# Alternating the PSUM bank of a unit's first dense item in a linear-attention phase

## The chip, the cores and the metric

The kernel runs on one core of one Trainium2 chip. The metric is the device time of one launch in microseconds, over the whole program: mixing, attention, MLP and routed experts. Before the change it is 2922.16 us, the median of three runs (2916.29 to 2923.81).

## What is computed

The input has 16 sequences of 512 tokens. A token mixing makes `h` from `x`; then a transformer block with linear attention, then a mixture of experts, each added to `h`. The change lies in the attention, whose core per sequence is (16 heads of 64, width 256):

```
h = _ln(x, g1, beta1)
q = _phi((h @ wq).reshape(b, s, H, DH), proj)      # elu(x @ proj) + 1
k = _phi((h @ wk).reshape(b, s, H, DH), proj)
v = (h @ wv).reshape(b, s, H, DH)
# causal: kv and ksum run along the tokens
num = q_t . kv ;  den = q_t . ksum + 1e-06 ;  out = num / den
x = x + out @ wo
```

## The kernel before

The program has three phases. `attention_phase` ends near 1,668 us, the MLP phase follows, and the routed experts end it. Only the first is touched. Every fp32 operand is split there into a high and a low fp16 part, and `three` (L498 to L502) makes each product of three matmuls, so the `nh`/`nl` in a row are the high and low part of the normalised rows, `sh`/`sl` those of the masked scores, `vh`/`vl` those of the values.

**The pipeline.** A *unit* is half a sequence, 256 tokens (`u = (i, h)`, two chunks `c` of 128 tokens), so there are 32 units. While unit u does its attention, the dense items of the *next* unit are computed and the mixing and norm of the unit after that. `unit` has eight slots `s`, and every engine runs the same list of steps (`run`), each doing its own part of a step in this fixed order. Nothing is scheduled at run time; engines meet at semaphores.

**The dense items.** The table `DENSE` spreads 13 items over the eight slots: eight feature items `f0` to `f7` (queries and keys, 12 matmuls of 256 columns each), four value items `v0` to `v3` (6 matmuls of 512 columns) and the output projection `p`. An item fills one of two PSUM banks, `pF[0]` and `pF[1]`, in turn: `n % 2`, with `n` counted through the table by `dense`. The count starts at 0 in each unit. As 13 is odd, `v3` (n = 12, slot 7) and the next unit's `f0` (n = 0, slot 0) are both in bank 0. Before an item is written, TensorE waits in `bank_free` until the item before it in its bank was read: a feature item is read by ScalarE (`rz`, L719) and last by VectorE (`fz`, L825), a value item by ScalarE (`vh`, L731) and last by VectorE (`vl`, L834).

**The boundary between two units** is where the change acts. TensorE's order there is: in slot 7 `v3`, the outputs (`pO`), a transposition (`pT`), the scores (`pS`, released by `sm` L851) and, where there is one, a state sum (`pKV`); then in slot 0 of the next unit `f0`, and the outputs of its first quarter. These outputs have two parts: a product with the state (`pO<-kvh,qkh`), which only chunks 1 to 3 have, and the product of values and masked scores (`pO<-vh,sh`), which waits for `sh`, for both parts of `sl` (VectorE's is L858) and for the values. VectorE's order in the same stretch is: in slot 7 `vl` of `v3`, division of the outputs (`dn`, `rd`, `on`; L875 to L883), the mask of the scores (`sm`, L851), the state (`kvt`, `kvacc`), then `sl` (L858). One slot earlier, at s = 6, it makes the norm's `tn` (L809) and `nl` (L815), with ScalarE's `nh` (L710) between; `f0` waits for both:

```
if n == 0:
    pe.wait_ge(nh_ready, units(w, DT, DT))
    pe.wait_ge(nl_ready, units(w, DT, DT))
bank_free(w, before)
```

I call the boundary inside a sequence (from unit (i, 0) to (i, 1)) A, and that between two sequences (from (i, 1) to (i + 1, 0)) B. At A the outputs have the state part and there is a state sum; at B neither.

Of the kernel before, what the change touches and what calls it, by code (L numbers as in the profile page):

```python
# [16 lines left out]
SEQS = 16  # L17
D = 256
DT = D // P
# [8 lines left out]
HALF = T // 2  # L28
XS = XK // 2
FEATS = 8  # L30
QK_GROUPS = 2 * QT * DT // 4
VALS = 4
# [3 lines left out]

DENSE = ((("f", 0),), (("f", 1), ("f", 2)), (("p", 0), ("f", 3)), (("v", 0), ("v", 1)), (("f", 4),),
         (("f", 5), ("f", 6)), (("f", 7), ("v", 2)), (("v", 3),))
OUT_BANK = 1
TURNS = 6 * CH - 2  # L40
EXP_LN_SET = 6
EXP_LN_SET = 6
# [4 lines left out]
WO_SCALE = 64.0  # L47
# [14 lines left out]
def after(u, n):  # L62

    return u[0] + (u[1] + n) // 2, (u[1] + n) % 2
# [27 lines left out]
def attention_phase(nc, io, w1_w, w2_w, mlp_loaded):  # L92
# [3 lines left out]
    with ExitStack() as ctx:  # L96
        def sb(name, shape, dt=F32):
            return ctx.enter_context(nc.sbuf_tensor(name, [P, *shape], dt))
# [8 lines left out]
        wo_h, wo_l = sb("wo_h", [QT, D], F16), sb("wo_l", [QT, D], F16)  # L107
# [142 lines left out]
        at = sb("at", [DT, HALF])  # L250

        def bank(name, dt=F32):
            return ctx.enter_context(nc.psum_tensor(name, [P, 2048 // (4 if dt == F32 else 2)], dt))

        pM = bank("pM")
        pF = [bank("pF0"), bank("pF1")]
# [43 lines left out]
        def run(engine, steps):  # L300


            def step(name, *args):
                if name in steps:
                    steps[name](*args)

            def use(u, what, bank, before):


                kind, n = what  # L310
                if kind == "p":
                    step("project", after(u, -1), before)
                elif kind == "f":
                    step("features", after(u, 1), n, bank, before)
                else:
                    step("values", after(u, 1), n, bank, before)

            def finish(u, what, bank):
                if what[0] == "f":
                    step("phi", after(u, 1), what[1], bank)  # L320
                elif what[0] == "p":
                    step("project_read", after(u, -1))

            def norm(u, s):

                if s < XS:
                    step("mix", u, s)
                    if s < XS - 1:
                        step("split", u, s + 1)
                    else:  # L330
                        step("h", u)
                elif s == 5:
                    step("x0", u)

            def norm_early(u, s):

                if s == 4:
                    step("mean", u)
                    step("centre", u)
                elif s == 5:  # L340
                    step("var", u)
                    step("rstd", u)
                elif s == 6:
                    step("normed", u)

            def dense(first, last):


                slots, before, n = [], {0: ("v", VALS - 1, 1), 1: ("f", FEATS - 1, 1)}, 0
                for s in range(8):  # L350
                    uses = [], []
                    for place, (kind, k) in enumerate(DENSE[s]):
                        if not ((kind == "p" and first) or (kind != "p" and last)):
                            uses[place].append(((kind, k), n % 2, before[n % 2]))
                            before[n % 2] = (kind, k, 0)
                        n += 1
                    slots.append(uses)
                return slots

            def unit(u, start=False, mix=True, last=False):  # L360
                i, h = u
                slots = dense(start, last)
                if mix:
                    step("split", after(u, 2), 0)
                for s in range(8):
                    c, g = 2 * h + s // 4, s % 4
                    early, late = slots[s]

                    summed = (c, g - 2) if g >= 2 and c < CH - 1 else (c - 1, g + 2) if g < 2 and c > 0 else None

                    if g < 2:
                        quad = (i, c, g + 2)
                    elif c < CH - 1:
                        quad = (i, c + 1, g - 2)
                    else:
                        quad = None if last else (i + 1, 0, g - 2)
                    for what in early:
                        use(u, *what)
                    step("outputs", i, c, g)

                    if g >= 2:
                        step("turn", i, c, g - 2)
                    elif c > 0:
                        step("turn", i, c - 1, g + 2)
                    elif not start:
                        step("turn", i - 1, CH - 1, g + 2)
                    for what in early:
                        finish(u, *what[:2])
                    if quad is not None:
                        step("scores", *quad)  # L390
                    step("outputs_split", i, c, g)
                    for what in late:
                        use(u, *what)
                    if summed is not None:
                        step("sums", i, *summed)
                    if g in (1, 2) and c < CH - 1:
                        step("keys", i, c, g - 1)
                    if quad is not None:
                        step("scores_split", *quad)
                    if summed is not None:  # L400
                        step("sums_split", i, *summed)
                    if mix:
                        norm_early(after(u, 2), s)
                        norm(after(u, 2), s)
                    for what in late:
                        finish(u, *what[:2])

            step("split", (0, 0), 0)
            for s in range(8):
                norm_early((0, 0), s)  # L410
                norm((0, 0), s)
            step("split", (0, 1), 0)
            slots = dense(True, False)
            for s in range(8):
                for what, bank_no, before in slots[s][0] + slots[s][1]:
                    use((0, -1), what, bank_no, before)
                    finish((0, -1), what, bank_no)
                norm_early((0, 1), s)
                norm((0, 1), s)
            for q in range(2):  # L420
                step("scores", 0, 0, q)
                step("scores_split", 0, 0, q)
            unit((0, 0), start=True)
            unit((0, 1))
            for i in range(1, SEQS - 1):
                unit((i, 0))
                unit((i, 1))
            unit((SEQS - 1, 0), mix=False)
            unit((SEQS - 1, 1), mix=False, last=True)
            step("turn", SEQS - 1, CH - 1, 2)  # L430
            step("turn", SEQS - 1, CH - 1, 3)
            step("project", (SEQS - 1, 1), ("p", 0, 1))
            step("project_read", (SEQS - 1, 1))

        block = ctx.enter_context(nc.Block())

# [60 lines left out]
        def _(pe):  # L497
            def three(out, wh, wl, mh, ml, first, last):  # L498

                pe.matmul(out, wh, mh, start=first, stop=False, skip_group_check=True)  # L500
                pe.matmul(out, wl, mh, start=False, stop=False, skip_group_check=True)  # L501
                return pe.matmul(out, wh, ml, start=False, stop=last, skip_group_check=True)  # L502

            def half(u):
                return slice(u[1] * HALF, (u[1] + 1) * HALF)
# [56 lines left out]
                               t == 0, t == DT - 1)  # L562
                mm.then_inc(v_done, 1)

            def project(u, before):
                bank_free(after(u, 2 - before[2] * (before[0] == "p")), before)
                pe.wait_ge(turn_read, output_turn(u[0], 2 * u[1] + 1, 3))
                for m in range(DT):
                    cols = slice(m * P, (m + 1) * P)
                    for t in range(QT):  # L570
                        mm = three(pF[OUT_BANK][:, m * HALF:(m + 1) * HALF], wo_h[:, t, cols], wo_l[:, t, cols],
                                   ot[:, 0, t, half(u)], ot[:, 1, t, half(u)], m == t == 0, t == QT - 1)
                mm.then_inc(at_done, 1)

# [206 lines left out]
        def _(ve):  # L781
# [53 lines left out]
                                               1 / V_SCALE, vh[:, c, heads, 0:DH],  # L835
                                               ALU.mult, ALU.subtract).then_inc(vl_ready, 1)

            def project_read(u):
                ve.wait_ge(at_done, units(u, 1, 1))
                if some(units(u, 1, 0)):  # L840
                    ve.wait_ge(at_stored, units(u, 16, 0))
                nc.vector.tensor_scalar(at[:, :, :], pF[OUT_BANK][:, :].rearrange("p (m n) -> p m n", m=DT), 1 / WO_SCALE, None,
                                        ALU.mult).then_inc(at_ready, 1)

            def scores(i, c, q):
# [1371 lines left out]
```

## Time and profile before

| | us |
|---|---|
| median of 3 runs (lowest, highest) | 2922.16 (2916.29, 2923.81) |
| the profiled execution | 2922.25 |
| its span in the trace | 2920.5 |
| TensorE busy | 2442.1 (84%) |
| VectorE busy | 1981.8 (68%) |
| GpSimd busy | 1665.0 (57%) |
| ScalarE busy | 1471.2 (50%) |

PE is TensorE (PEld its weight loads), DVE VectorE, ACT ScalarE, POOL GpSimd. A row's line is that of the code; matmuls all have the lines of `three`, so they are told apart by the tiles they write. "Idle before" is what the engine stood still before an instruction, with the releaser behind the arrow; the releaser "issue" means that the profile shows no semaphore event for it. PEclk is the granted clock of TensorE as a share of 2.4 GHz: 1.00 is that level, 0.50 is 1.2 GHz.

### The profile page before, as it was taken

The numbers are of one execution on the slowest core, as the hardware profiler recorded it, in microseconds if no ns is written. First come the engines' busy times: TensorE is split into PE (matmuls) and PEld (weight loads), VectorE is DVE, ScalarE is ACT, GpSimd is POOL, SyncE is SP. The second block draws the span as 40 slices with busy tenths as digits, with TensorE's granted clock in tenths as the row PEclk, the third lists the DMA queues.
The fourth block names the chain that finished last, engine by engine and source line by source line (L and its number), as shares of the span: only waits on it lengthen the run. The fifth ranks groups of instructions, "written<-read, shape, count | busy, mean of one in ns | idle before, by whom it ended". The sixth has DMA issues, their size and how long they took to land. (4 is left out here: it accounts for less than half of the span.)

```text
span 2920.5 us, 61365 instructions
## 1 busy us (share of the span) xinstructions
PE 2442.1 (84%) x22832; PEld 1757.8 (60%) x22832; DVE 1981.8 (68%) x4227; ACT 1471.2 (50%) x2731; POOL 1665.0 (57%) x1627
## 2 busy tenths in 40 slices
PE   4899999999999999999999759888888888955444
PEld 3677777877787778777877524444444444434333
DVE  3667777777777777777777538777877787852222
ACT  3656666666656566656666434444444344311111
POOL 1555556565655555555555324556556556657776
PEclk8999999999999999999999879999999999987666
DMA  4111111111111111111110121112112111004554
GB/s 141 38 41 38 35 44 34 41 38 41 38 42 34 45 34 41 34 45 34 42 38 16 35 72 59 37 41 69 37 37 72 39 37 51 16 22 99 86 87 64
DMA packets 110742, 138.14 MB, mean 47 GB/s; under 512 B 20720, under 2 KB 77040, under 8 KB 110448
## 3 DMA queue, kind: packets, MB, share of 16 engines
q1 hardware_dynamic: 84816, 110.94, 12.3%
q0 software_dynamic: 23552, 21.17, 4.7%
q8 instruction: 185, 3.03, 0.5%
q10 hardware_dynamic: 2080, 2.10, 0.2%
q14 instruction: 109, 0.89, 0.1%
HBM read 81.22 MB, written 53.04 MB: 46 GB/s over the span
## 5 line engine op out<-in xcount | busy, mean ns | idle before, releaser
L929 POOL TENSOR_TENSOR qkl<-fz,qkh 128x512 f16<-128x512 f32 x256 | 297.1, 1160 | 282.1 <-DVE qkh L828 282.1
L500 PE MATMUL pF<-nh,qk_h 128*128 128x256 f16 x1024 | 289.2, 282 | 62.7 <-DVE vl L834 57.2
L941 POOL TENSOR_TENSOR ol<-on,oh 128x256 f16<-128x256 f32 x256 | 188.4, 736 | 208.5 <-ACT oh L765 208.5
L1802 POOL DMA_INDIRECT list_dram<-entry,slot_u x256 | 257.4, 1005 | 75.3 <-issue 74.8
L502 PE MATMUL pF<-nl,qk_h 128*128 128x256 f16 x1024 | 289.2, 282 | 0.0
L501 PE MATMUL pF<-nh,qk_l 128*128 128x256 f16 x1024 | 289.1, 282 | 0.0
L749 ACT ACTIVATE ot<-pT 128x512 f16<-128x512 f16 x256 | 149.9, 586 | 182.8 <-PE pT L659 182.8
L742 ACT ACTIVATE sh<-sm 128x512 f16<-128x512 f32 x256 | 159.5, 623 | 105.6 <-DVE sm L851 105.6
L948 POOL TENSOR_TENSOR kvl<-kvacc,kvh 128x260 f16<-128x260 f32 x192 | 156.9, 817 | 91.3 <-ACT kvh L773 89.9
L1783 POOL TENSOR_TENSOR al<-az,ah 128x512 f16<-128x512 f32 x64 | 79.1, 1236 | 224.1 <-DVE ah L1575 224.0
L875 DVE TENSOR_SCALAR dn<-pO 128x4 f32<-128x4 f32 x256 | 40.4, 158 | 233.0 <-PE pO L502 232.8
L825 DVE SCALAR_TENSOR_TENSOR fz<-pF,ez 128x512 f32<-128x512 f32 x256 | 174.8, 683 | 34.8 <-ACT ez L725 33.3
L935 POOL TENSOR_TENSOR sl<-sm,sh 128x512 f16<-128x512 f32 x128 | 153.7, 1200 | 75.4 <-ACT sh L742 75.4
L719 ACT ACTIVATE rz<-pF 128x512 f32<-128x512 f32 x256 | 151.1, 590 | 83.1 <-PE pF L502 81.8
L500 PE MATMUL pS<-qkh 64*128 64x128 f16 x1024 | 189.0, 220 | 2.6 <-DVE sm L851 2.6
L501 PE MATMUL pS<-qkh,qkl 64*128 64x128 f16 x1024 | 186.4, 218 | 0.0
L502 PE MATMUL pS<-qkl,qkh 64*128 64x128 f16 x1024 | 186.3, 218 | 0.0
L851 DVE TENSOR_TENSOR sm<-pS,mask 128x512 f32<-128x512 f32 x256 | 174.3, 681 | 5.2 <-PE pS L502 5.2
L923 POOL TENSOR_TENSOR xl<-xs,xh 128x512 f16<-128x512 f32 x128 | 148.0, 1157 | 37.4 <-ACT xh L674 37.3
L725 ACT ACTIVATE ez<-rz 128x512 f32<-128x512 f32 x256 | 161.3, 630 | 8.2
L500 PEld LDWEIGHTS pF<-nh,qk_h 128*128 128x128 f16 x1024 | 102.7, 100 | 92.3 <-issue 61.6
L828 DVE CAST qkh<-fz 128x512 f16<-128x512 f32 x256 | 148.5, 580 | 8.8
(320 smaller groups left out, 8897.7 us busy)
## 6 DMA issues: line engine op xcount, KB each, us to landing
xs<-in_x SPq DMA_DIRECT2D x128, 256.0 KB, 2.7
h_dram<-hT SPq DMA_DIRECT2D x32, 256.0 KB, 2.2
x_dram<-x SPq DMA_DIRECT2D x32, 256.0 KB, 2.2
at_dram<-at SPq DMA_DIRECT2D x32, 256.0 KB, 2.2
x0b<-x_dram SPq DMA_DIRECT2D x16, 512.0 KB, 4.5
atb<-at_dram SPq DMA_DIRECT2D x16, 512.0 KB, 5.6
hb_in<-h_dram SPq DMA_DIRECT2D x16, 512.0 KB
xrow_dram<-xt SPq DMA_DIRECT2D x32, 256.0 KB, 2.2
```

Of the source, the lines that this page charges most:

```text
L500: pe.matmul(out, wh, mh, start=first, stop=False, skip_group_check=True)
L501: pe.matmul(out, wl, mh, start=False, stop=False, skip_group_check=True)
L502: return pe.matmul(out, wh, ml, start=False, stop=last, skip_group_check=True)
L725: nc.scalar.activation(ez[:, s, :, :], rz[:, s, :, :], ACT.Exp, scale=-1.0, bias=-math.log(PHI_DOWN)).then_inc(e_ready, 1)
L742: nc.scalar.activation(sh[:, q, :, :], sm[:, n % 2, :, :], ACT.Copy).then_inc(sh_ready, 1)
L825: nc.vector.scalar_tensor_tensor(fz[:, s, :, :], pF[bank_no][:, :].rearrange("p (b n) -> p b n", b=2), 0.0, ez[:, s, :, :], ALU.max, ALU.a ...
L851: nc.vector.tensor_tensor(sm[:, n % 2, :, :], pS[:, :].rearrange("p (a b) -> p a b", b=P), mask[:, :].unsqueeze(1).broadcast_to([P, 4, P]) ...
L929: nc.gpsimd.tensor_tensor(qkl[:, pair:pair + 2, cols], fz[:, n % 2, :, :], qkh[:, pair:pair + 2, cols], ALU.subtract).then_inc(fl_ready, 1)
L935: nc.gpsimd.tensor_tensor(sl[:, q, :, :], sm[:, 0, :, :], sh[:, q, :, :], ALU.subtract).then_inc(sl_ready[0], 1)
L941: nc.gpsimd.tensor_tensor(ol[:, n % 2, :], on[:, n % 2, :, :].rearrange("p a b -> p (a b)"), oh[:, n % 2, :], ALU.subtract).then_inc(ol_re ...
L948: nc.gpsimd.tensor_tensor(kvl[:, pairs, :, :], kvacc[:, pairs, :, :], kvh[:, pairs, :, :], ALU.subtract).then_inc(kvl_ready, 1)
L1802: nc.gpsimd.indirect_dma_start(io["list_dram"], bass.IndirectOffsetOnAxis(slot_u[:, c, k:k + 1], 0), entry[:, c, k, :], None, bounds_check ...
```

## The change

The bank count of a unit starts at the unit's parity: at 0 for the first half of a sequence and at 1 for the second. So `v3` of a unit and `f0` of the next are in different banks, at A and at B. The initial uses of the banks are told accordingly: `f0` waits for the `vl` of the last unit's `v2`, and the first item of the other bank (`f1`) for that of `v3`; before, `f0` waited for `v3` and `f1` for the last unit's `f7`. As the projection's bank now depends on the unit, `project` and `project_read` are given it. On every engine all instructions stay in the same order, and their number stays: only bank numbers and these two semaphore waits differ.

```diff
-OUT_BANK = 1
+LAST_BANK = 1
...
-                    step("project", after(u, -1), before)
+                    step("project", after(u, -1), bank, before)
...
-            def dense(first, last):
+            def dense(turn, first, last):
-                slots, before, n = [], {0: ("v", VALS - 1, 1), 1: ("f", FEATS - 1, 1)}, 0
+                slots, n = [], turn % 2
+                before = {n: ("v", VALS - 2, 1), 1 - n: ("v", VALS - 1, 1)}
...
             def unit(u, start=False, mix=True, last=False):
                 i, h = u
-                slots = dense(start, last)
+                slots = dense(h, start, last)
...
-            slots = dense(True, False)
+            slots = dense(-1, True, False)
...
-                        mm = three(pF[OUT_BANK][:, m * HALF:(m + 1) * HALF], wo_h[:, t, cols], wo_l[:, t, cols],
+                        mm = three(pF[bank_no][:, m * HALF:(m + 1) * HALF], wo_h[:, t, cols], wo_l[:, t, cols],
...
-                nc.vector.tensor_scalar(at[:, :, :], pF[OUT_BANK][:, :].rearrange("p (m n) -> p m n", m=DT), 1 / WO_SCALE, None,
+                nc.vector.tensor_scalar(at[:, :, :], pF[bank_no][:, :].rearrange("p (m n) -> p m n", m=DT), 1 / WO_SCALE, None,
```

## Rows read from the trace of the kernel before

**Rows 1.** Waits of TensorE between 100 and 1,800 us: total, times, longest.

```profile
PE pF L500 <- DVE vl L834: 57.2, 30, 2.1
PE pO L500 <- issue: 18.1, 26, 2.1
...
PE pO L500 <- DVE sl L858: 7.2, 6, 1.5
```

**Rows 2.** Busy time of a stretch between two boundaries, from A on.

```profile
core 0: us, PE busy (x) PEld busy (x) DVE busy (x) ACT busy (x) POOL busy (x), PEclk, DMA share, GB/s
...
744.10:785.60 41.50, 41.00 (x490) 34.54 (x490) 30.53 (x64) 27.02 (x56) 25.87 (x27) 1.00 0.16 46
```

**Rows 3.** VectorE in order of time at boundary A: start, duration, instruction, idle before.

```profile
740.02 0.48 DVE L815 SCALAR_TENSOR_TENSOR nl<-tn,b,nh 128x256 f16<-128x256 f32 x1 [0.25 <-ACT nh L710]
740.44 0.69 DVE L834 SCALAR_TENSOR_TENSOR vl<-pF,vh 128x512 f16<-128x512 f32 x1
...
743.28 0.68 DVE L858 TENSOR_TENSOR sl<-sm,sh 128x512 f16<-128x512 f32 x1
```

**Rows 4.** TensorE at A: `f0`'s first and last matmul, the outputs' parts.

```profile
741.28 0.27 PE L500 MATMUL pF<-nh,qk_h 128*128 128x256 f16 x1 [1.74 <-DVE vl L834]
...
742.48 0.27 PE L502 MATMUL pF<-nl,qk_h 128*128 128x256 f16 x1
742.59 0.22 PE L500 MATMUL pO<-kvh,qkh 128*128 128x130 f16 x1
...
742.87 0.22 PE L502 MATMUL pO<-kvl,qkh 128*128 128x130 f16 x1
744.17 0.19 PE L500 MATMUL pO<-vh,sh 128*128 128x65 f16 x1 [1.08 <-issue]
```

**Rows 5.** VectorE at boundary B.

```profile
788.40 1.77 DVE L815 SCALAR_TENSOR_TENSOR nl<-tn,b,nh 128x256 f16<-128x256 f32 x2
790.09 0.68 DVE L834 SCALAR_TENSOR_TENSOR vl<-pF,vh 128x512 f16<-128x512 f32 x1
...
791.42 0.68 DVE L851 TENSOR_TENSOR sm<-pS,mask 128x512 f32<-128x512 f32 x1
792.80 0.69 DVE L858 TENSOR_TENSOR sl<-sm,sh 128x512 f16<-128x512 f32 x1 [0.70 <-ACT sh L742]
```

**Rows 6.** TensorE at B: `f0`'s first and last matmul, then the outputs.

```profile
790.92 0.37 PE L500 MATMUL pF<-nh,qk_h 128*128 128x256 f16 x1 [2.07 <-DVE vl L834]
...
793.22 0.42 PE L502 MATMUL pF<-nl,qk_h 128*128 128x256 f16 x1
793.85 0.21 PE L500 MATMUL pO<-vh,sh 128*128 128x65 f16 x1 [0.22 <-issue]
```

**Rows 7.** Busy time by stretch, for the granted clock (PEclk) after boundaries.

```profile
142.40:145.70 3.30, 3.21 (x19) 2.45 (x20) 2.66 (x7) 2.15 (x5) 1.28 (x2) 0.50 0.01 2
195.40:200.10 4.70, 4.70 (x39) 3.69 (x40) 2.40 (x6) 2.62 (x5) 2.54 (x4) 0.50 0.19 56
343.70:347.10 3.40, 3.40 (x30) 2.78 (x27) 2.43 (x5) 2.52 (x6) 1.68 (x3) 0.50 0.01 2
398.20:401.70 3.50, 3.50 (x19) 2.52 (x18) 1.28 (x3) 1.26 (x3) 2.71 (x3) 0.52 0.27 76
739.50:742.90 3.40, 1.66 (x19) 1.51 (x18) 3.05 (x9) 2.21 (x5) 0.50 (x1) 1.00 0.00 0
790.90:793.30 2.40, 2.38 (x12) 1.63 (x12) 1.67 (x4) 1.57 (x3) 0.67 (x1) 0.50 0.00 0
793.80:794.20 0.40, 0.35 (x7) 0.38 (x8) 0.00 (x0) 0.40 (x1) 0.40 (x1) 0.50 0.00 0
```

**Rows 8.** `f0`'s first matmul at the first and the fifth A, the fourth and last B.

```profile
142.49 0.37 PE L500 MATMUL pF<-nh,qk_h 128*128 128x256 f16 x1 [1.74 <-DVE vl L834]
543.33 0.27 PE L500 MATMUL pF<-nh,qk_h 128*128 128x256 f16 x1 [1.74 <-DVE vl L834]
494.01 0.37 PE L500 MATMUL pF<-nh,qk_h 128*128 128x256 f16 x1 [2.07 <-DVE vl L834]
1582.88 0.37 PE L500 MATMUL pF<-nh,qk_h 128*128 128x256 f16 x1 [2.07 <-DVE vl L834]
```

**Rows 9.** TensorE at an early B: `f0` at full clock, then the outputs.

```profile
393.53 0.27 PE L500 MATMUL pF<-nh,qk_h 128*128 128x256 f16 x1 [2.07 <-DVE vl L834]
396.46 0.19 PE L500 MATMUL pO<-vh,sh 128*128 128x65 f16 x1 [1.47 <-DVE sl L858]
```

**Rows 10.** VectorE before A, at the last place where it waits for TensorE.

```profile
726.07 0.16 DVE L875 TENSOR_SCALAR dn<-pO 128x4 f32<-128x4 f32 x1 [0.50 <-PE pO L502]
```

More of the change, by code:

```diff
@@ L321, in finish @@
                 elif what[0] == "p":
-                    step("project_read", after(u, -1))
+                    step("project_read", after(u, -1), bank)
             def norm(u, s):
@@ L431, in run @@
             step("turn", SEQS - 1, CH - 1, 3)
-            step("project", (SEQS - 1, 1), ("p", 0, 1))
-            step("project_read", (SEQS - 1, 1))
+            step("project", (SEQS - 1, 1), LAST_BANK, ("p", 0, 1))
+            step("project_read", (SEQS - 1, 1), LAST_BANK)
         block = ctx.enter_context(nc.Block())
@@ L563, in values, with project @@
                 mm.then_inc(v_done, 1)
-            def project(u, before):
+            def project(u, bank_no, before):
                 bank_free(after(u, 2 - before[2] * (before[0] == "p")), before)
@@ L836, in values, with project_read @@
                                                ALU.mult, ALU.subtract).then_inc(vl_ready, 1)
-            def project_read(u):
+            def project_read(u, bank_no):
                 ve.wait_ge(at_done, units(u, 1, 1))
```

## The prediction

> **What bounds the kernel now.** I read TensorE's waits first. In the attention phase the longest is the one that the change removes: `f0` waits 30 times for `vl`, 57.2 us in all [rows 1], 2.0% of the time. Between boundaries TensorE bounds: it is busy 41.00 of 41.50 us, at PEclk 1.00 [rows 2], and VectorE waits for it (0.50 us at 726.07 [rows 10]). So what TensorE loses there is lost for good.
>
> At the boundaries it is the other way round, and there I read VectorE in order of time. At A it makes `nl`, `vl`, divides, masks, updates the state and makes `sl`, with no gap after `nl` [rows 3]. Nothing in that chain waits for `f0`: VectorE's first use of `f0` (`fz`) stands behind the outputs' division, which stands behind `sl`. TensorE meanwhile stops twice: before `f0` (1.74 us) and again before `pO<-vh,sh` (1.08 us [rows 4]). The profile names no releaser for that second stop, but the matmul starts 0.21 us after `sl` ends (743.28 + 0.68 = 743.96, against 744.17), and six of its like name `sl` [rows 1]. At B the same: 2.07 us before `f0`, then 0.22 before the outputs [rows 6]; `sl` ends at 792.80 + 0.69 = 793.49, after waiting 0.70 us for ScalarE's `sh` [rows 5]. `sh` waits for `sm`, and `sm` for VectorE's turn, not for `f0`. **The wait for the bank is the first of two waits in a row, and the second is set by VectorE alone.**
>
> **What the change does, part by part.**
>
> 1. *`f0` starts earlier, but little.* It also needs `nl` of its unit, which VectorE makes right before `vl`. At A `nl` ends at 740.02 + 0.48 = 740.50 and `vl` at 740.44 + 0.69 = 741.13 [rows 3], so `f0` moves from 741.28 to about 740.65, by 0.63 us. At B `nl` ends at 788.40 + 1.77 = 790.17 and `vl` at 790.09 + 0.68 = 790.77 [rows 5], so `f0` moves from 790.92 to 790.32, by 0.60 us. Over 30 boundaries 30 x 0.615 = 18.5 us of the 57.2 go; 38.7 stay, as a wait for `nl`.
>
> 2. *Those 18.5 us come back before the outputs.* `sl` ends when it did. At A TensorE still starts `pO<-vh,sh` at 744.17: the stop there grows from 1.08 to about 1.7 us. Gain: 0.
>
> 3. *At B a rest is gained.* `pO<-vh,sh` begins at 793.85, just behind `f0`, which ran at half clock (its last matmul 793.22 + 0.42 = 793.64 [rows 6]). With `f0` out of the way it could begin 0.21 us after `sl`, at 793.70: 0.15 us. The half clock lasts until about 794.15 [rows 7], so of 793.85 to 794.15 half, another 0.15 us, could be gained if the clock were up. Together 0.3 us x 15 = 4.5 us at most.
>
> 4. *The bank's other users cost nothing.* `f1` now waits for the `vl` of `v3`, done a whole slot before. `f0` waits for `vl` of `v2`, which VectorE makes before `tn` and `nl`. Items inside a unit alternate as before. No instruction moves on any engine, no queue is passed, no DMA changes.
>
> 5. *The clock.* This is the term that decides. TensorE drops to 1.2 GHz after these stops. From 494 us on it drops at each B (`f0` begins with a matmul of 0.37 us at the first and the last of them [rows 8]; 0.27 is that of the full clock [rows 4]), exactly over `f0`: 2.4 us at 0.50, then the first outputs, and up again [rows 7]. There it is nearly free, because the 1.2 us that twelve matmuls lose (their starts are 2.30 / 11 = 0.21 us apart [rows 6] and at A 1.20 / 11 = 0.11 [rows 4]) lie inside the wait for `sl`. And `f0` is also what brings the clock back: TensorE works almost without pause from 790.92 into the outputs. After the change `f0` runs from 790.32 to 791.6, and then TensorE stands still about 2.1 us until 793.70, with nothing dense behind it. At A it stands still 1.1 us before `f0` and, as the state part ends near 742.4, 1.8 us after it. The clock then drops when the outputs and the long TensorE-bound stretch begin, and recovery takes place there.
>    What such a spell costs is in the early rows, where it fell on bound work: 142.4 to 145.7, 343.7 to 347.1 and 398.2 to 401.7, each some 3.4 us at 0.50, so 3.4 / 2 = **1.7 us**. Lower bound 0 (the clock stays up, as at 739.5 to 742.9 with 1.74 us idle), upper bound the 4.7 us at 0.50 of 195.4 to 200.1, so 2.35 us [rows 7]. I take 1.7 for all 30 boundaries, since the early B at 393.53 is what every B becomes: `f0` at full clock, then a stop (1.47 us there, 2.1 to come), then the spell [rows 9].
>    What before pays for the same thing comes off. Steady sequences take (1582.88 - 494.01) / 11 = 98.99 us; the first four, from A at 142.49 to A at 543.33, take 400.84 [rows 8], 4.9 us over 4 x 98.99. With the 4.5 us of step 3 that is 9.4.
>
> **Sum.** 30 x 1.7 - 9.4 = +41.6 us. The profiled execution took 2922.25 us, as good as the median of 2922.16. Forecast: **2964 us**. A sequence would take 98.7 + 2 x 1.7 = 102.1 us instead of 98.99. Its own range goes from two boundaries in three paying (20 x 1.7 - 9.4 = +25) to each paying and a few paying 2.35, +50: 2947 to 2972.
>
> The Trainium skill (TensorE: Matmul & The Clock Gate, HAM oscillation) describes a loop whose recurring wait lets the clock fall so that every tile starts cold; rows 7 agree, and by it all 30 boundaries pay. The same page (Loop structure matters more than you think) says that a VectorE copy out of PSUM does not break the clock; by that the time would stay, and that is the second rival.
>
> **Rivals.**
>
> - *Mixed.* The clock falls at one boundary per sequence, or only as often as in the first four sequences. For: not all early boundaries show a spell. 15 x 1.7 - 9.4 = +16; at the early rate 15 x (4.9 / 4) - 4.9 = +13.5. About 2937 us. Chance 0.25.
> - *No change.* The waits move and the clock behaves as now, because the stops are short and their sum is the old one (2.8 us at A before and after). 0 to -4.5 us: 2918 to 2922. Against: in the steady state the clock falls at B in every sequence already. Chance 0.19.
> - *Faster: the boundary was TensorE's.* If `sl` came as early as `f0` allows, the whole 57.2 us would go: 2865 us; with `nl` as the limit, 18.5 us: 2904. It decides if `sl` moves with `f0`. Against: VectorE is without a gap from `nl` to `sl` at A, and at B waits only for ScalarE's `sh`. For: reading one bank while TensorE fills the other might shorten a VectorE operation, which no row shows. Chance 0.06.
>
> The Trainium skill (PSUM — Partial Sum Buffer, Summary: rules for kernel authors) advises to read one bank while matmuls fill another, which is what the change does; by that advice alone the faster rival would win.
>
> **The numbers.** A difference of 0.3% (8.8 us) is about what a measurement can tell. Forecast 0.50 and mixed 0.25 are slower by more (with mixed under 8.8 us in a few cases), no change 0.19, faster 0.06, of which 0.05 by over 0.3%. So faster 0.05, same 0.22, slower 0.73. The range reaches from the no-change case to the top of the forecast: 2920 to 2972.
>
> **What would show it.** The wait of `f0` for `vl` gone, and one for `nl` of 1.1 us at A and 1.5 at B in its place; the stop before `pO<-vh,sh` 1.7 and 2.1 us; `sl` at the same distance behind `nl`; PEclk 1.00 over `f0` at B and 0.50 over some 3.4 us behind the outputs of both boundaries; a steady sequence near 102 us. The prediction is wrong if the sequence takes 99 us with these waits (the clock was no matter), or less than 98.5 (`sl` came earlier).

## The result and the profile after: slower by 1.05%

The changed kernel takes 2953.02 us (median of 4 runs, 2945.56 to 2956.55) where the kernel before takes 2922.98 us (4 runs, 2916.29 to 2925.40): a ratio of 1.0105, with a 95% interval of 1.009 to 1.0119. Ratios here and below are estimated without two executions, one of the kernel before (3671.67 us) and one of old_wait_new_banks (3581.71 us), in which the granted clock was 0.64 and 0.67 on average instead of 0.93. The profiled execution took 2953.64 us, its span is 2951.9 us. A second comparison (changed_again, below) gave 1.0094 (1.0075 to 1.0113).

**The waits.** TensorE's waits between 100 and 1,800 us of the changed kernel: total us, times, longest.

```profile
PE pO L501 <- DVE sl L859: 34.8, 18, 2.2
PE pO L501 <- issue: 28.1, 17, 2.1
PE pF L501 <- issue: 21.4, 15, 1.4
PE pF L501 <- ACT nh L711: 16.0, 15, 1.1
```

The 57.2 us for `vl` of [rows 1] are gone. 21.4 + 16.0 = 37.4 us of them stay as 30 waits for the norm's `nh` and `nl`, and the waits before `pO`, 18.1 + 7.2 = 25.3 us in [rows 1], are now 62.9. They grew by more than the 19.8 us that left `f0`, because `f0` no longer runs at half clock at B: the stop before the outputs is 2.12 us there where it was 0.22 (below).

**Boundary A** in the changed kernel, TensorE and then VectorE in order of time (answers to [rows 4] and [rows 3]):

```profile
849.53 0.27 PE L501 MATMUL pF<-nh,qk_h 128*128 128x256 f16 x1 [1.07 <-ACT nh L711]
...
853.09 0.19 PE L501 MATMUL pO<-vh,sh 128*128 128x65 f16 x1 [1.75 <-issue]
```

```profile
848.94 0.48 DVE L816 SCALAR_TENSOR_TENSOR nl<-tn,b,nh 128x256 f16<-128x256 f32 x1 [0.25 <-ACT nh L711]
849.36 0.69 DVE L835 SCALAR_TENSOR_TENSOR vl<-pF,vh 128x512 f16<-128x512 f32 x1
...
852.20 0.68 DVE L859 TENSOR_TENSOR sl<-sm,sh 128x512 f16<-128x512 f32 x1
```

`f0` now starts while VectorE still makes `vl`, 0.11 us after `nl` ended (849.42). Nothing moved on VectorE: from the start of `nl` to that of `sl` it is 852.20 - 848.94 = 3.26 us, as in [rows 3] (743.28 - 740.02), and TensorE goes on 0.21 us after `sl` ends, as before.

**Boundary B**, answers to [rows 6] and [rows 5]:

```profile
900.80 0.27 PE L501 MATMUL pF<-nh,qk_h 128*128 128x256 f16 x1 [1.42 <-issue]
902.00 0.27 PE L503 MATMUL pF<-nl,qk_h 128*128 128x256 f16 x1
...
904.38 0.19 PE L501 MATMUL pO<-vh,sh 128*128 128x65 f16 x1 [2.12 <-DVE sl L859]
```

```profile
898.93 1.76 DVE L816 SCALAR_TENSOR_TENSOR nl<-tn,b,nh 128x256 f16<-128x256 f32 x2
900.62 0.68 DVE L835 SCALAR_TENSOR_TENSOR vl<-pF,vh 128x512 f16<-128x512 f32 x1
...
903.33 0.69 DVE L859 TENSOR_TENSOR sl<-sm,sh 128x512 f16<-128x512 f32 x1 [0.70 <-ACT sh L743]
```

`f0` runs at full clock (0.27 a matmul; 0.37 and 0.42 in [rows 6]) and is done near 902.3, then TensorE stands still for 2.12 us. From the end of `sl` (903.33 + 0.69 = 904.02) to the outputs it is 0.36 us, the same as in [rows 5] and [rows 6] (793.49 to 793.85).

**The clock.** Busy time by stretch around these two boundaries; the number before the DMA share is PEclk.

```profile
core 0: us, PE busy (x) PEld busy (x) DVE busy (x) ACT busy (x) POOL busy (x), PEclk, DMA share, GB/s
849.50:853.00 3.50, 1.81 (x18) 1.52 (x18) 3.27 (x8) 2.05 (x5) 0.87 (x2) 1.00 0.00 0
854.00:857.30 3.30, 3.30 (x26) 2.61 (x24) 2.99 (x7) 1.99 (x5) 2.25 (x3) 0.51 0.31 81
857.40:860.00 2.60, 2.60 (x39) 2.37 (x37) 0.00 (x0) 1.32 (x4) 2.60 (x4) 0.99 0.02 5
900.70:904.40 3.70, 1.49 (x13) 1.15 (x14) 2.56 (x6) 2.12 (x5) 1.18 (x2) 1.00 0.00 0
905.20:908.50 3.30, 3.30 (x23) 2.48 (x22) 2.16 (x5) 2.02 (x4) 1.59 (x2) 0.51 0.29 79
908.60:911.00 2.40, 2.40 (x36) 2.10 (x34) 0.33 (x2) 0.71 (x3) 2.33 (x3) 0.99 0.00 0
```

The clock is up over the boundary itself and down about a microsecond behind it, for 3.3 us in which TensorE is busy all the time. Such a stretch at 1.2 GHz is a *spell*; one costs 3.3 / 2 = 1.65 us here. In the steady state before, [rows 7], nearly all of the spell lay over `f0` and inside the wait for `sl`.

What a sequence costs is then a matter of counting. `f0`'s first matmul at four B in a row:

```profile
701.56 0.27 PE L501 MATMUL pF<-nh,qk_h 128*128 128x256 f16 x1 [1.43 <-issue]
...
800.38 0.27 PE L501 MATMUL pF<-nh,qk_h 128*128 128x256 f16 x1 [1.42 <-issue]
...
900.80 0.27 PE L501 MATMUL pF<-nh,qk_h 128*128 128x256 f16 x1 [1.42 <-issue]
...
1002.94 0.27 PE L501 MATMUL pF<-nh,qk_h 128*128 128x256 f16 x1 [1.42 <-issue]
```

They are 98.82, 100.42 and 102.14 us apart, with no spell, one and two in between. Over the whole phase I count 19 spells on such work behind the 30 boundaries, 8 behind A and 11 behind B; in the trace of changed_again (below) 21, and one more over `f0` at the first A.

**Where the 31 us are.** The last write of `at`, the end of the attention phase, starts 25.6 us later than before: L842 in the kernel before, L843 in the changed one (behind the durations in ns: the first and the last start in us).

```profile
L842 DVE TENSOR_SCALAR at<-pF x32: 678/680/691, 162.2 to 1668.7; 128x512 f32<-128x512 f32 x32
```

```profile
L843 DVE TENSOR_SCALAR at<-pF x32: 678/679/690, 164.8 to 1694.3; 128x512 f32<-128x512 f32 x32
```

By the spells: 19 x 1.65 = 31.4, less the 4.9 us that the first four sequences of before lost, less 15 x 0.17 = 2.6 for the shorter undisturbed sequence (98.82 against 98.99), is 23.9, an estimate against the 25.6. The other 5.8 us of the difference of the spans (31.4) lie behind the attention phase. In the second pair of traces, before_again and changed_again, the phase ended 27.9 us later (1,668.0 and 1,695.9) and the rest was 1.8 us shorter, so the rest differs by some microseconds in either direction, and nothing shows that its 5.8 us are the change's.

### The profile page after: what moved, and what is told of

Same layout as the page of the kernel before. It is cut to its first block and busy times, and to the rows that moved or that the text cites. A ratio compares the mean times of both kernels' runs of the same rounds, so it can differ in the third digit from the quotient of the medians.

```text
span 2951.9 us, 61365 instructions
## 1 busy us (share of the span) xinstructions
PE 2448.5 (83%) x22832; PEld 1760.2 (60%) x22832; DVE 1977.4 (67%) x4227; ACT 1471.9 (50%) x2731; POOL 1666.5 (56%) x1627
## 5 line engine op out<-in xcount | busy, mean ns | idle before, releaser
L501 PE MATMUL pF<-nh,qk_h 128*128 128x256 f16 x1024 | 283.4, 277 | 43.3 <-issue 21.4
L502 PE MATMUL pF<-nh,qk_l 128*128 128x256 f16 x1024 | 282.1, 275 | 0.0
L503 PE MATMUL pF<-nl,qk_h 128*128 128x256 f16 x1024 | 281.4, 275 | 0.0
L501 PE MATMUL pO<-vh,sh 128*128 128x65 f16 x1024 | 120.3, 194 | 67.7 <-DVE sl L859 34.8
L501 PE MATMUL pM<-xh,tok_h 128*128 128x256 f16 x512 | 151.1, 295 | 15.3 <-POOL xl L924 15.3
```

## The experiments

Two theories were open. **The slow clock**: the change only moves a wait, and the moved wait lets the clock drop where TensorE bounds. **The banks**: reading one bank while another is written, or the projection's changing bank, costs something. The runs fall into three groups, each on a chip of its own, with the kernel before measured beside them. On the chip of the first group (old_wait_new_banks, new_banks_filled, old_banks_filled, sl_earlier) it takes 2952.0 us (31 runs), on the other two 2921 to 2925; only ratios within a group are compared. For the attention phase, where all of this plays, the traces are compared too.

### The old wait on the new banks

```diff
-                before = {n: ("v", VALS - 2, 1), 1 - n: ("v", VALS - 1, 1)}
+                before = {n: ("v", VALS - 1, 1), 1 - n: ("v", VALS - 1, 1)}
```

> The changed kernel with the alternating banks, but f0 waits for the vl of v3 again, as before the change (it does not need to). Theory, the slow clock: the stops are then those of the kernel before (1.7 and 2.1 us before f0, about 1.1 and 0.2 us before the outputs), f0 again stands right ahead of the outputs, most sequences take 99 us, and the time is that of the kernel before, 2918 to 2926 us. Rival, the banks themselves (the alternation or the projection's changing bank costs something): 2945 to 2957 us, as the changed kernel.

Measured: 2949.18 us, a ratio of 0.9992 (0.9977 to 1.0008) to the kernel before on that chip. The absolute forecast missed, because the chip is slower for both; the ratio is the theory's. The waits are those of before, and where the sequences have settled the spell is over `f0`, with the clock up behind it:

```profile
893.97 0.37 PE L501 MATMUL pF<-nh,qk_h 128*128 128x256 f16 x1 [2.07 <-DVE vl L835]
...
896.91 0.21 PE L501 MATMUL pO<-vh,sh 128*128 128x65 f16 x1 [0.22 <-issue]
```

```profile
893.90:896.30 2.40, 2.33 (x12) 1.66 (x12) 1.64 (x4) 1.52 (x3) 0.67 (x1) 0.50 0.00 0
897.30:900.50 3.20, 3.20 (x43) 2.78 (x41) 2.38 (x6) 1.91 (x5) 1.19 (x2) 1.00 0.34 87
```

So the banks alone cost nothing: the whole loss hangs on when `f0` starts. Its attention phase ends at 1,672.7 us, 4 us behind before's, as it settles later: from 494 us on the spell lies over `f0` at each B in the first trace of before, from 692 us in before_again, and from 894 us here.

### Holding the clock: the stops filled

Both edits add matmuls into columns of the outputs' bank that nobody reads; the program's results don't depend on them. In new_banks_filled 14 stand before the first outputs of a unit. In old_banks_filled 8 stand there, and 10 before `f0`, behind a wait until the division has read that bank; the second part of the cut below is that run's.

```diff
+                if g == 0 and c % 2 == 0:
+                    for k in range(14):
+                        pe.matmul(out[:, 264:504], qk_h[:, 0, 0:P], qk_h[:, 0, 0:240], start=first and k == 0, stop=True,
+                                  skip_group_check=True)
                 if g % 2 == 0:
...
+                    if some(count(i, 16, 8 * h - 1)):
+                        pe.wait_ge(on_ready, count(i, 16, 8 * h - 1))
+                    for k in range(10):
+                        pe.matmul(pO[0][:, 264:504], qk_h[:, 0, 0:P], qk_h[:, 0, 0:240], start=k == 0, stop=True,
+                                  skip_group_check=True)
                 if n == 0:
                     pe.wait_ge(nh_ready, units(w, DT, DT))
```

> The changed kernel, with 14 matmuls of 240 columns that nobody reads (into free columns of the outputs' bank, about 1.4 us at full clock) put into the stop of TensorE before the first outputs of a unit. Theory, the slow clock: TensorE works through most of the stop, the granted clock stays at 1.00 behind all boundaries, every sequence takes 98.7 to 98.9 us and the time falls by 19 spells x 1.65 = 31 us to about 2922, or a little below the kernel before (2915 to 2923). Rival, another cost of the change on the path (a later sl, a conflict of the banks): the clock is 1.00, but the time stays above 2940. Rival, filling cannot hold the clock: spells remain and the time stays near 2950.

> The kernel before, with unread matmuls of 240 columns in both stops of a boundary: 10 before f0 and 8 before the outputs. With the clock held in both, this and the filled changed kernel compare the banks alone. Theory (sl of VectorE sets when TensorE goes on, whichever bank f0 has): both take the same within 3 us, 2913 to 2921 here, 5 to 9 us under the kernel before, which is what its own spells cost. Rival (the earlier f0 is worth something once the clock is out of the way): this one is slower than the filled changed kernel by up to 18 us.

Measured against the same before: 2942.90 us, 0.9972 (0.9953 to 0.9991) with the new banks; 2943.43 us, 0.9966 (0.9949 to 0.9982) with the old. Alike, and both under the kernel before. With the old banks no spell is left between 150 and 1,620 us and a sequence takes 98.65 us; with the new ones four spells were left, over `f0` at A, where the stop ahead of it was not filled, and most sequences without one take 98.65. The rival with up to 18 us for the earlier `f0` falls.

In the second group the changed kernel had both stops filled (10 and 14), beside the unedited kernels.

> The kernel before, unedited, for its trace on the chip of this call (the earlier call's chip took 2952 us for it, not 2922). Theory: the attention phase ends near 1,669 us as in the first trace, with sequences of 99 us once settled, and what a chip adds lies in the MLP phase and behind, which the change does not touch. Rival: the attention phase itself is longer on such a chip, 1,690 us or more.

> The changed kernel, unedited, against the kernel before on one chip. Theory, the slow clock: attention ends 20 to 30 us later than in before_again, with spells of 3.3 us at half clock on the work behind 15 to 30 of the boundaries, and the time is 1.007 to 1.012 of before, as in the first comparison. Rival, that the 30 us were a chip's difference: 0.998 to 1.003.

> The changed kernel with unread matmuls in both stops of a boundary, 10 before f0 and 14 before the outputs (new_banks_filled had only the second and kept four spells behind boundary A). Theory: no spell is left, every sequence takes 98.65 us as in old_banks_filled, attention ends within 2 us of 1,657 us. Rival: with the stop ahead of f0 filled too, f0 or sl comes later or earlier and the sequence differs from 98.65 by over 0.3 us, so the banks have a value of their own.

Measured: before 2924.79 us (13 runs; before_again, a single run, 2921.82, with attention ending at 1,668.0 us, as in the first trace, and sequences of 98.8 to 99.1 us once settled); changed_again 2950.99, ratio 1.0094 (1.0075 to 1.0113); new_banks_filled_twice 2914.02, ratio 0.9966 (0.9952 to 0.9979). The same stretch of the attention phase, first of changed_again, then of new_banks_filled_twice:

```profile
640.00:1130.00 490.00, 453.15 (x5214) 373.38 (x5215) 354.45 (x746) 302.43 (x601) 277.84 (x289) 0.97 0.13 38
```

```profile
640.00:1130.00 490.00, 478.62 (x5647) 399.73 (x5645) 368.45 (x774) 314.30 (x626) 288.87 (x300) 1.00 0.13 39
```

In 490 us VectorE, which got no added work, does 774 instructions where it did 746. The sequence is 98.65 us with either set of banks once no clock is lost, and the attention phase ends at 1,658.4 us with the new and at 1,656.2 us with the old. (The longer time on the first group's chip lies behind that phase: the span of old_banks_filled is 2944.5 us, that of new_banks_filled_twice 2907.2.)

The same holds without added matmuls. In before_again the kernel before had no spell from 402 to 690 us, and its sequences were 98.80 us long there, against 98.82 for the changed kernel without a spell:

```profile
402.00:690.00 288.00, 268.89 (x3205) 223.82 (x3202) 216.79 (x455) 184.16 (x368) 167.88 (x175) 1.00 0.13 39
```

```profile
444.48 0.27 PE L500 MATMUL pF<-nh,qk_h 128*128 128x256 f16 x1 [1.74 <-DVE vl L834]
...
543.28 0.27 PE L500 MATMUL pF<-nh,qk_h 128*128 128x256 f16 x1 [1.74 <-DVE vl L834]
```

**The change by itself is worth nothing, and the 1% is all clock.**

The 0.17 us from 98.82 to 98.65 are the added matmuls' own. With them right ahead of the outputs TensorE goes on 0.21 us after `sl` at B too, instead of 0.36 (new_banks_filled_twice, 887.68 + 0.69 = 888.37):

```profile
887.68 0.69 DVE L870 TENSOR_TENSOR sl<-sm,sh 128x512 f16<-128x512 f32 x1 [0.70 <-ACT sh L754]
```

```profile
888.58 0.19 PE L501 MATMUL pO<-vh,sh 128*128 128x65 f16 x1 [0.53 <-issue]
```

### Which stop brings the clock down

The changed kernel with the 10 matmuls before `f0` alone, so that only the stop before the outputs is left.

> The changed kernel with 10 unread matmuls in the stop before f0 alone; the stop before the outputs stays at 1.75 us (A) and 2.12 us (B). It tells which of the two stops brings the clock down. Theory (both together; f0's work is spread over the stops, and it is how little TensorE does around the long stop that counts): fewer spells than the 24 of changed_again, at B more than at A, 3 to 15 left, attention ends between 1,662 and 1,683 us. Rival, the stop right before the outputs alone does it: 20 or more spells, attention ends at 1,690 us or more. Rival, the stop before f0 alone: no spell behind any boundary, attention ends near 1,658 us.

Measured: 2962.51 us in a single run, where before takes 2921.07 (9 runs). The first rival holds, and my theory of both stops together falls: most sequences take 102.0 to 102.4 us, there are 24 spells, three of them of twice the length, and attention ends at 1,708.9 us. At the B near 604 us:

```profile
600.21 0.27 PE L501 MATMUL pF<-nh,qk_h 128*128 128x256 f16 x1 [0.30 <-issue]
...
603.79 0.19 PE L501 MATMUL pO<-vh,sh 128*128 128x65 f16 x1 [2.12 <-DVE sl L866]
```

```profile
604.00:610.80 6.80, 6.80 (x49) 5.12 (x46) 2.41 (x6) 2.42 (x5) 4.47 (x5) 0.50 0.14 39
```

`f0` follows the added work after 0.30 us and runs at full clock, then comes the stop, and behind it 6.8 us at half clock, twice the usual length. A stop of 2.12 us before the outputs is enough to bring the clock down behind it, with 10 added matmuls ahead of `f0` as without. Work ahead of the stop did not protect. Whether it makes things worse isn't shown: this is one execution, and the two traces of the changed kernel differ from each other too (19 and 21 spells).

### Bringing `sl` forward

If `sl` ends the boundary, an earlier `sl` should shorten it. In a unit's last slot VectorE masks the scores first, divides the outputs, makes `sl`, and only then `vl` and the state sum; ScalarE makes `sh` before `oh`. This needs the new banks, since `vl` of `v3` comes later and `f0` must not wait for it.

```diff
+                    lead = s == 7 and quad is not None
+                    dve, act_ = lead and "x0" in steps, lead and "rstd" in steps and "x0" not in steps
+                    if dve:
+                        step("scores", *quad)
+                        step("outputs", i, c, g)
+                        step("scores_split", *quad)
                     for what in early:
                         use(u, *what)
-                    step("outputs", i, c, g)
+                    if not dve:
+                        step("outputs", i, c, g)
...
+                    if act_:
+                        step("scores_split", *quad)
                     step("outputs_split", i, c, g)
```

> The changed kernel, with another order in a unit's last slot: VectorE masks the scores (sm) first, then divides the outputs, then makes sl, and only then vl of v3 and the state sum; ScalarE makes sh before oh. Theory: sl is the last to arrive at the boundary, and it comes 1.2 to 1.4 us earlier; the stop before the outputs shrinks from 1.75 and 2.12 us to about 0.5 and 0.9. With the clock staying up, 30 x 1.25 = 37 us less than with the clock held, so 2880 to 2890; if the spells stay as they are, 2915 to 2920. Rival, TensorE then waits for the transposition's oh and ol or for f0's nl: the gain is under 10 us beside the changed kernel.

Measured: 2944.55 us, ratio 0.9979 (0.9962 to 0.9997) on the slow chip; attention ends at 1,666.5 us, against 1,694.3 for the changed kernel. The stops before the outputs are 0.29 (A) and 0.78 us (B), but an undisturbed sequence is only 0.95 us shorter, 97.87, where the theory had 2 x 1.25. So neither the theory nor the rival holds in full: behind A TensorE meets a new wait of 1.69 us for `xl`, because the state sum, with it ScalarE's `kvh`, and the `xh` behind it in the queue come late:

```profile
745.21 0.27 PE L510 MATMUL pM<-xh,tok_h 128*128 128x256 f16 x1 [1.69 <-POOL xl L933]
```

There are 11 spells in this trace, all behind A and each beginning within 0.8 us of the end of that wait (the expectation of sl_and_xh_earlier, below, says 8). None begins right behind the outputs. Which of the stops ahead of it brings the clock down there isn't separated.

Two repairs followed. First the state sum goes ahead of `vl`, with the stops filled (10 and 3):

```diff
                         step("scores_split", *quad)
+                        if summed is not None:
+                            step("sums", i, *summed)
                     for what in early:
```

> The changed kernel with VectorE's sl early in a unit's last slot as in sl_earlier, but with the state sum ahead of vl, and 10 unread matmuls before f0 and 3 before the outputs. In sl_earlier the sequence without spells took 97.87 us: B gained 1.3 us, but at A TensorE then waited 1.69 us for xl, because kvacc and with it ScalarE's kvh and xh came late. Theory: with the state sum ahead of vl that wait is gone and a sequence takes 96.0 to 96.6 us, attention ends near 1,625 us, and the time is 0.985 to 0.989 of before. Rival: vl of v3 now delays the next outputs' division and a new wait takes most of it; 97.5 us or more a sequence.

Measured: 2894.26 us, ratio 0.9895 (0.9878 to 0.9913). A sequence takes 97.29 us, more than the 96.0 to 96.6 expected, and the ratio misses its 0.985 to 0.989 by a little: the wait for `xl` is 1.12 us instead of gone. ScalarE still makes `xh` after `kvh`, for which it stands still 1.06 us:

```profile
633.66 0.42 ACT L796 ACTIVATE kvh<-kvacc 128x260 f16<-128x260 f32 x1 [1.06 <-DVE kvacc L931]
633.98 0.61 ACT L697 ACTIVATE xh<-xs 128x512 f16<-128x512 f32 x1
```

Then the next unit's first `xh` and `xl` are made before `kvh` and `kvl`, with and without the added matmuls:

```diff
-                if mix:
+                if start:
                     step("split", after(u, 2), 0)
...
+                    if s == 7 and after(u, 1)[0] < SEQS - 1:
+                        step("split", after(u, 3), 0)
                     if summed is not None:
                         step("sums_split", i, *summed)
```

> sl_earlier_filled, and the next unit's first xh and xl are made before kvh and kvl in a unit's last slot instead of behind them. In sl_earlier_filled TensorE waited 1.12 us for xl behind each A. Theory: that wait goes and nothing takes its place, a sequence takes 96.2 us (97.29 - 1.12), attention ends near 1,620 us, and the time is 0.983 to 0.987 of before. Rival: kvl comes late instead, or xl now delays ol; a sequence takes 97 us or more.

> The same without any unread matmul. Theory: with the stops down to 1.07 and 1.43 us before f0 and about 0.3 and 0.8 us before the outputs the clock rarely falls at B and sometimes at A (sl_earlier had 8 spells behind A and none behind B): 0 to 8 spells of 1.65 us, so 0 to 13 us over the filled version. Rival: spells behind most boundaries, 25 us or more over the filled version.

Measured beside a before of 2921.07 us (9 runs): 2876.62 us, ratio 0.9845 (0.9826 to 0.9864), filled; 2878.06 us, 0.9851 (0.9834 to 0.9867), not filled. A sequence takes 96.17 us in both, as forecast. In the settled part of the attention phase of the unfilled one, TensorE's longest waits are

```profile
PE pF L514 <- issue: 21.4, 15, 1.4
PE pF L514 <- ACT nh L724: 15.0, 14, 1.1
PE pO L514 <- DVE sl L872: 12.4, 16, 1.0
```

and four spells are left (one near 141 us and three later, each in a sequence of 97.2 to 97.3 us), all over `f0` at A, behind the stop of 1.07 us. With the stop before the outputs at 0.3 and 0.8 us the clock holds by itself behind all other boundaries. This version is 1.5% faster than the kernel before; against the changed kernel it wasn't measured side by side.

## Why the prediction was right

The forecast was 2964 us, in a range of 2920 to 2972; 2953 was measured, and the mechanism is the one forecast. The range alone says little, since it also holds the rivals "mixed" and "no change"; the forecast's own range was 2947 to 2972.

1. *`f0` starts earlier, but little*: right. Forecast were waits for `nl` of 1.1 us at A and 1.5 at B; 1.07 and 1.42 were found.
2. *It comes back before the outputs*: forecast 1.7 and 2.1 us, found 1.75 and 2.12, with `sl` at the same distance behind `nl`. The runs with filled stops, 98.65 us a sequence with either banks, show that nothing else depends on it.
3. *A rest gained at B*, up to 0.3 us a sequence in two halves: one half came. The sequence without a spell is 98.82 instead of 98.99, 0.17 us less, for the first outputs at full clock. The other half, an earlier start of the outputs once `f0` is out of the way, did not: they start 0.36 us behind `sl` at B in the changed kernel as in the old, so `f0` had not been in their way. The term should have been 2.6 us instead of 4.5.
4. *The bank's other users cost nothing*: shown by the old wait on the new banks, 0.9992.
5. *The clock*: the right term, mis-sized in number. The price of a spell was forecast at 1.7 us and measured at 1.65. The count was forecast at all 30 boundaries and is 19 in one trace and 21 in the other. So the sum should have been 20 x 1.65 - 7.5 = +25.5 for the attention phase instead of +41.6. That is the forecast's own lower bound (two boundaries in three, +25). The mixed rival (one boundary per sequence, +16) is on the other side. Of the attention phase's 25.6 us it is nearer; of the 30.0 us of the medians the forecast is, by 11.6 against 14; of the 26.2 us of the second comparison the rival is again. That the forecast came out ahead of it by the first medians is in part luck, as 5.8 us of the difference of the first two traces lie behind the attention phase.

The price was right although two of its three rows were misread. Only the spell of 398.2 to 401.7 fell on bound work: from the B before it to the B behind it (393.53 in [rows 9] to 494.01 in [rows 8]) it is 100.48 us, 1.7 over the 98.8 of a sequence without a spell. Those of 142.4 and 343.7 lay over `f0` and the outputs of A, mostly inside the wait for `sl`:

```profile
343.49 0.27 PE L500 MATMUL pF<-nh,qk_h 128*128 128x256 f16 x1 [1.74 <-DVE vl L834]
...
346.48 0.26 PE L500 MATMUL pO<-vh,sh 128*128 128x65 f16 x1
```

The sequence around the second of them, from the B at 294.27 to that at 393.53, took 99.26 us, 0.5 over.

The reason given for step 5 was right in one half. That a long stop directly before TensorE-bound work brings the clock down there is shown by first_stop_filled. That it falls at every boundary ("the early B at 393.53 is what every B becomes") was extrapolated from one row: the drop falls behind some boundaries and not behind others with the very same waits. The sequences of 98.82 us have them too, which by the prediction's own sign ("wrong if the sequence takes 99 us with these waits") speaks against it for those sequences, while those near 102.1 us are as forecast. And rows 7, which the prediction says agree with every boundary paying, hold one that did not: 739.5 to 742.9 at 1.00, behind a stop of 1.74 us. In the loop that the Trainium skill describes there (TensorE: Matmul & The Clock Gate, HAM oscillation) the wait of each round is a longer one than the 1 to 2 us here, so it was no ground for all 30.

The traces show a pattern in which boundaries are spared. Spells come at several boundaries in a row, and at A as at B each begins later behind the first `pO<-vh,sh` than the one before it there. In the changed kernel they begin, by the granted clock, 0.77, 1.00, 0.86, 1.34, 1.24, 1.69 and 1.52 us behind it from 198.69 on, then the boundary near 552 us is spared; 0.95, 0.87, 1.21, 1.11, 1.58, 1.42, 1.87 and 1.72 us from 854.04 on, then the one near 1,258 us. changed_again has two such runs of eight. Why they begin later each time, and why a boundary is then spared, isn't settled by these runs.

The second rival's ground, by the Trainium skill (TensorE: Matmul & The Clock Gate, Loop structure matters more than you think), was that a VectorE copy out of PSUM does not break the clock. The page says it of a loop whose next matmuls follow immediately. That is not so here, where TensorE waits 1.75 and 2.12 us for VectorE's result, and the clock fell behind 19 of 30 boundaries. The rival "faster" is excluded: `sl` did not move with `f0`, and no VectorE operation on the banks got shorter (`vl` 0.68 to 0.69 us in both).

## What to carry to other kernels

When two waits stand in a row on an engine, removing the first is worth only what the releaser of the second allows; look for that releaser's own queue (here VectorE from `nl` to `sl`) and shorten that, which, together with making `xh` and `xl` earlier, gave 1.5%. A stop of TensorE has a second price, the clock behind it: it matters whether the slow spell falls on work inside a wait, where it is nearly free (0.17 us a sequence here), or on work that bounds (1.65 us), so a change that only moves a wait can cost 1%. Unread matmuls in the stops are a quick way to tell the two prices apart.

## What the runs showed of the hardware

The clock of TensorE was at 1.2 GHz for 3.3 to 3.4 us at a time (6.8 us in a few places) after stops of 1.69 to 2.17 us, and in new_banks_filled and sl_and_xh_earlier after a few of 1.07 us. It fell between 0.5 us before the end of such a stop and 1.9 us behind it. Filling the stop before `f0` alone did not help (24 spells, attention ended at 1,708.9 us in its one execution, against 1,694.3 and 1,695.9 with 19 and 21), filling both removed every such spell. And the kernel before had settled into a state in which the spell is nearly harmless: sequences of 98.99 us with the spell over `f0`. Before it settled, the longest of its first four sequences (from A at 142.49 to A at 243.88 us) took 2.4 us more. I had not expected the placing of a spell to be worth more than its length. The same kernel took 1% longer on one of the chips than on two others (2952.0 and 2921.1 to 2924.8 us, 31 and 22 runs), as much as this whole change.
